# Adding the weighted state of one first-level unit in four by an accumulating DMA from GpSimd

## The reference, cut to what matters

```python
def _ssm(x, xw, dtw, dtb, Al, Dv, g, be):
    ...
    dA = jnp.exp(delta[..., None] * A)
    dBx = delta[..., None] * Bs[:, :, None, :] * xt[..., None]
    def step(h, inp):
        da, dbx, c = inp
        h = h * da + dbx
        return (h, jnp.einsum('bdn,bn->bd', h, c))      # sum over the 16 states n
    ...
    y = ys.transpose(1, 0, 2) + xt * Dv
    return _layernorm(y, g, be)
...
y1 = _ssm(fx1, ...1) + flip(_ssm(flip(fx1), ...2)) + y1_
```

## Time and profile before

| | |
|---|---|
| median of 3 executions | 4336.49 us (4335.89 to 4338.08) |
| profiled execution | 4338.19 us, of which 4336.4 us lie between the first and the last instruction |
| busy share | PE 71%, DVE 82%, ACT 59%, POOL 77% |
| mean granted clock of TensorE | 0.825 |

### The profile page before, as it was taken

One profiled execution on the slowest core, in us unless ns is written; L12 is line 12 of the kernel. 1 busy time (PEld: TensorE's weight loads), 2 busy tenths in 40 slices (PEclk: granted clock), 3 DMA queues, 4 the chain that ended last, 5 costly groups with the idle time before them and its releaser, 6 DMA issues.

```text
span 4336.4 us, 51200 instructions
## 1 busy us (share of the span) xinstructions
PE 3086.1 (71%) x11852; PEld 1449.5 (33%) x11852; DVE 3559.6 (82%) x4199; ACT 2552.1 (59%) x6006; POOL 3338.1 (77%) x1908
## 2 busy tenths in 40 slices
PE   6977767777776778767777876777877777876511
PEld 3433333333332433333333333333333333332200
DVE  2178888888888888888888888888888888898777
ACT  4466665655665665666656666665676566565432
POOL 0069597895969879696896969789596996969798
PEclk8988788888888888887888888888887888888755
DMA  1036354463544446354453534446253454635444
GB/s 40 1 125 206 117 179 147 157 200 108 197 140 157 165 147 204 115 190 146 157 186 125 201 129 167 149 159 209 99 196 131 168 174 137 205 113 182 165 157 174
DMA packets 187260, 663.95 MB, mean 153 GB/s; under 512 B 22736, under 2 KB 24672, under 8 KB 186976
## 3 DMA queue, kind: packets, MB, share of 16 engines
q1 hardware_dynamic: 186976, 661.47, 45.0%
HBM read 639.76 MB, written 21.63 MB: 153 GB/s over the span
## 4 chain that ended last, share of the span: by engine, by line
POOL 28%; issue 23%; DVE 17%; PE 13%; ACT 11%; DMA 6%; DVEq 1%; POOLq 1%; SPq 0%; ACTq 0%
POOL bx L1342 12%; POOL y L1370 7%; DMA bb<-bc_rows 6%; DVE h L581 6%; POOL h L1365 5%; ACT diag L1085 5%; PE pconv L822 4%; DVE slot_c L572 3%; POOL bx L1345 2%; PE pm L848 2%; DVE rs L528 1%; DVE rs L520 1%; ACT slot_b L1200 1%; PE pm L839 1%; POOL delta L1310 1%
## 5 line engine op out<-in xcount | busy, mean ns | idle before, releaser
L822 PE MATMUL pconv<-pad,diag 128*128 128x512 f16 x8064 | 2052.6, 412 | 132.7 <-DVE xn L506 66.9
L1370 POOL TENSOR_TENSOR y<-y,h 128x1024 f32<-128x1024 f32 (+2 forms) x672 | 1335.6, 1987 | 153.9 <-DVE h L581 131.2
L1200 ACT ACTIVATE slot_b<-delta,nega 128x512 f32<-128x512 f32 (+1 forms) x1280 | 804.3, 640 | 1010.6 <-DVE slot_c L572 1009.0
L822 PEld LDWEIGHTS pconv<-pad,diag 128*128 128x128 f16 x8064 | 826.1, 104 | 1328.6 <-issue 423.3
L1342 POOL TENSOR_TENSOR bx<-bb,u 128x1024 f32<-128x1024 f32 x512 | 1219.4, 2382 | 19.9 <-DMA bb<-bc_rows 19.9
L572 DVE TENSOR_TENSOR_SCAN slot_c<-slot_b,bx 128x512 f32<-128x512 f32 (+1 forms) x1024 | 954.2, 956 | 296.1 <-POOL bx L1342 255.4
L581 DVE TENSOR_TENSOR h<-slot_c,cb 128x512 f32<-128x512 f32 x1280 | 860.4, 673 | 36.6 <-POOL y L1370 36.6
L572 DVE TENSOR_TENSOR_SCAN slot_c<-slot_b,slot_c,bx 128x512 f32<-128x512 f32 x512 | 663.7, 1296 | 74.8 <-ACT slot_b L1200 18.7
L1310 POOL TENSOR_TENSOR delta<-delta,rs 128x512 f32<-128x512 f32 (+1 forms) x96 | 111.8, 1164 | 464.6 <-DVE rs L530 464.6
L1365 POOL TENSOR_TENSOR h<-h 128x512 f32<-128x512 f32 (+3 forms) x384 | 361.2, 941 | 98.3 <-DVE h L551 80.7
L1085 ACT ACTIVATE diag<-id,chi 128x128 f16<-128x128 f16 x1344 | 426.6, 386 | 10.7 <-PE pconv L822 10.1
(11 more groups left out here) (168 smaller groups left out, 3555.2 us busy)
## 6 DMA issues: line engine op xcount, KB each, us to landing
bb<-bc_rows SPq DMA_DIRECT2D x592, 512.0 KB, 4.5
cb<-bc_rows SPq DMA_DIRECT2D x592, 512.0 KB, 4.4
xr<-in_x SPq DMA_DIRECT2D x16, 1024.0 KB, 4.9
out<-ob SPq DMA_DIRECT2D x16, 1024.0 KB
bc_rows<-rows SPq DMA_DIRECT2D x64, 64.0 KB, 1.6
w<-in_w SPq DMA_DIRECT2D x2, 256.0 KB
wc<-in_wc SPq DMA_DIRECT2D x2, 256.0 KB
bc_rows<-rows SPq DMA_DIRECT2D x16, 32.0 KB, 1.5
```

Of the source, the lines that this page charges most:

```text
L822: ins = nc.tensor.matmul(bank(pconv, k), w, pad[:, t, part, rows:rows + 16, dx:dx + W], start=first and m == 0, stop=last and m == 2)
L1200: ins = nc.scalar.activation(slot_b[:, o:o + w], delta[:, so + c:so + c + w], ACT.Exp, scale=nega[:, st, n0 + n:n0 + n + 1])
L1370: pool.tensor_tensor(yv, yv, src[:, 0] if len(src.shape) == 3 else src, ALU.add).then_inc(q_y.sem, 1)
```

## The change

In units 6, 10, 14, 18, 22, 26, 30 and 34 (states 1, 5, 9 and 13 of each direction) POOL no longer makes the pass L1370. In its place it issues a DMA from the `h` slot to `ob[:, d, :]`: a plain copy for state 1, an accumulating one (`accum_op=add`) for states 5, 9 and 13. Before it POOL waits for the weighing as before, and for the DMA of four units earlier (for the first of an image: for the store of `ob` of the image before, a wait that DVE's `output` loses). Each of these two waits is carried by an increment of a semaphore of its own. DVE's `weigh` waits for the DMA's arrival where the slot three products back was sent. `norm_centre` of the first level waits for the DMAs too, and subtracts the mean of both sums: a second product, of `ob`, is accumulated onto that of y.

```diff
+def by_dma(q):
+    u, _ = PRODUCTS[q]
+    return UNITS[u][0] == 1 and UNITS[u][3] % 4 == 1
+def added(q):
+    return sum(not by_dma(v) for v in range(q))
+def sent(q):
+    return sum(by_dma(v) for v in range(q))
...
-        q_y = Count("q_y", NP)
+        q_y = Count("q_y", added(NP))
+        q_acc = Count("q_acc", 16 * sent(NP))
...   # DVE, weigh
                 if p == 0 and q >= HR:
-                    dve.wait_ge(q_y.sem, q_y.at(i, q - HR + 1))
+                    if by_dma(q - HR):
+                        dve.wait_ge(q_acc.sem, q_acc.at(i, 16 * sent(q - HR + 1)))
+                    else:
+                        dve.wait_ge(q_y.sem, q_y.at(i, added(q - HR + 1)))
...   # DVE, output
-                if hh == 0:
-                    dve.wait_ge(ob_free.sem, ob_free.at(i + 1, 0))
...   # PE, norm_centre
-                nc.tensor.matmul(o, cen[:, :], src, start=True, stop=True).then_inc(n_yc.sem, 1)
+                    nc.tensor.matmul(o, cen[:, :], src, start=True, stop=True).then_inc(n_yc.sem, 1)
+                    return
+                pe.wait_ge(q_acc.sem, q_acc.at(i, 16 * sent(NORM_NEEDS[k])))
+                nc.tensor.matmul(o, cen[:, :], src, start=True, stop=False)
+                nc.tensor.matmul(o, cen[:, :], ob[:, d, c0:c0 + n], start=False, stop=True).then_inc(n_yc.sem, 1)
...   # POOL, gather
+                if by_dma(q):
+                    pool.wait_ge(q_pr.sem, q_pr.at(i, weighed(q)))
+                    pool.sem_inc(pool_held, 1)
+                    if sent(q) == 0:
+                        pool.wait_ge(ob_free.sem, ob_free.at(i + 1, 0))
+                        pool.sem_inc(pool_held, 1)
+                        pool.dma_start(ob[:, d, :], h[:, q % HR, 0:ln]).then_inc(q_acc.sem, 16)
+                    else:
+                        pool.wait_ge(q_acc.sem, q_acc.at(i, 16 * sent(q)))
+                        pool.sem_inc(pool_held, 1)
+                        if UNITS[k][3] == 1:
+                            pool.dma_start(ob[:, d, :], h[:, q % HR, 0:ln]).then_inc(q_acc.sem, 16)
+                        else:
+                            pool.dma_start(ob[:, d, :], h[:, q % HR, 0:ln], accum_op=ALU.add).then_inc(q_acc.sem, 16)
+                    return
```

More of the change, by code:

```diff
@@ L281, in build @@
         sp_held = sem("sp_held")
+        pool_held = sem("pool_held")
         ch_out = [Count(f"ch_out{n}", 16 * (NCH // 2)) for n in range(2)]
@@ L873, in norm_centre @@
                     pe.wait_ge(n_o.sem, n_o.at(i, STEPS[k]))
-                pe.wait_ge(q_y.sem, q_y.at(i, NORM_NEEDS[k]))
+                pe.wait_ge(q_y.sem, q_y.at(i, added(NORM_NEEDS[k])))
                 o = norm_psum(k)[0][:, 0:cols]
@@ L1368, in gather @@
                 if q:
-                    pool.wait_ge(q_y.sem, q_y.at(i, q))
+                    pool.wait_ge(q_y.sem, q_y.at(i, added(q)))
                 pool.tensor_tensor(yv, yv, src[:, 0] if len(src.shape) == 3 else src, ALU.add).then_inc(q_y.sem, 1)
```

## The result

The changed kernel takes 4381.5 us (median of 4 executions, 4371.96 to 4388.93) against 4336.19 us before (4333.34 to 4338.08): 1.0104 times the time before, 95% interval 1.0083 to 1.0125. It is 45 us slower where 45 us faster was predicted. The profiled execution took 4384.01 us, 4382.2 of it between the first and the last instruction, at a mean granted clock of 0.826 (0.825 before).

The account below looks back on a forecast made before the run. POOL was taken to set the pace from unit 17 to 31, and the chain to norm 4's root in the bridge. 16 images x (2.7 - 5.5) = -45 us gave 4293, 4292 for a median; range 4247 to 4375.

Parts of the forecast that it names:

- What bounds the kernel: Units 17 to 31: POOL sets the pace, busy 63.92 of 64.00 us; in the bridge, DVE waits for norm 4's root.
- The price of a send, c = 1.3 us: On POOL: waiting, two semaphore increments and issuing the DMA cost 1.3 us, the middle between 0.39 and 2.35.
- s: On POOL: time saved per sent gather, 2.3 - 1.3 = 1.0 us.
- rival 1: On POOL: a cheap issue of 0.4 to 0.8 us, saving 1.5 to 1.9 per send; 4247 to 4267 us, chance 0.18.
- Where the saving reaches DVE, 5.5 us per image: 1.0 us each behind gathers 6, 18, 22 and 26, 1.5 behind gather 14, nothing behind 30 and 34.
- the 24 credited to L520: DVE's L520 beside gather 14 falls from 2.19 to 0.68 us, so 1.5 us per image count.
- 3.0 us were credited to gathers 18, 22 and 26: DVE's scans wait behind these gathers, so the saving of 1.0 us counts at each.
- The second sum, 2.7 us per image in the bridge: Bridge, PE ahead of spread 4: direction 1's two products cost 1.8 to 3.6 us, middle 2.7; direction 0's cost nothing.
- The slot of h, "just hidden": From gather 18 to unit 21's first weighing: issue and landing take 7.3 us of the 7.56 available.
- a sign that it is wrong: DVE's weighing waiting for the DMA, a gap of 2 us or more, or no growth of the wait before L625.
- The load of bb, left to the range: POOL's next rows: needed 5.9 us after issue behind a sent gather, median landing 4.5; possible delay left to the range.
- Rival 2: At DVE's weighing: the DMA lands after 8 us, not 6; stalls of 96 us, time 4388 us, chance 0.2.

## Why the prediction was wrong, point by point

1. **What bounds the kernel**: right as far as it went. POOL set the pace, and without sends the relief is worth 87 us.
2. **The price of a send, c = 1.3 us**: too high. The accumulate takes 0.87 us of POOL, the copy 0.60. At gather 18 the next pass begins 0.60 us after the send (time order of POOL above) and takes 0.27 us longer than the one before it. So s is 2.3 - 0.87 = 1.4 rather than 1.0, just under the 1.5 to 1.9 of rival 1. This error alone would have made the kernel faster than forecast, not slower.
3. **Where the saving reaches DVE, 5.5 us per image**: the places early in the image were right, the late ones were eaten. Take the image whose count starts at the norm step of 1541.42 (before: 1526.64). DVE after is ahead of before by 0.5 us ahead of the first send and by 2.2 us at weighing 24, so gather 6 gave 1.7, credited 1.0. L538 behind gather 14 takes 0.68 us at 1664.53 where L520 took 2.19, as predicted; but just ahead of it 1.75 us had been lost where DVE waited for chunk 4 (2.38 us for ACT at 1660.04). That wait comes from PE's clock. PE's products for this chunk, first after and then before:

```profile
1653.61 1.91 PE L882 MATMUL pm<-f,wbc 128*32 128x512 f32 x2 [3.75 <-DVE o L631]
1641.02 1.05 PE L863 MATMUL pm<-f,wbc 128*32 128x512 f32 x2 [1.19 <-DVE o L610]
```

After 3.75 us of idling they run at a granted clock of 0.50, after 1.19 us at 1.00. At this place it is so in 14 of 16 images after and in 2 before, and DVE's wait behind it is 33.7 us in sum instead of 12.6: 21 us that no term of the prediction has, nearly the 24 credited to L520. By weighing 44 the lead is 1.94 us. From there on 3.0 us were credited to gathers 18, 22 and 26; instead DVE lost 3.4 and stood 1.44 behind at the last weighing. The run without sends shows too that the credit was generous: with the whole 2.35 us saved it gave 5.5 us, not the 9 that my way of counting gives.
4. **The second sum, 2.7 us per image in the bridge**: the way was right, the size a little high. Centre 4 to norm 4 grew from 8.56 us to 10.09, the mean over 16 bridges by 1.7 us and that of the whole bridge by 2.0, the wait before the norm step from 57.6 to 84.0 us (101 was written). The run without products puts all four at 48 us against 43, but for direction 0 nothing was counted; 23 of the 57 us by which the span fell without products lie outside the bridge, so a small cost may stand there, and the nearness of the two sums is in part luck.
5. **The slot of h, "just hidden"**: failed. The estimated landing was 6.0 us, the real one 8.4, and the forecast named 7 us as the point from which it decides. The estimate started from the median load of bb, and where few or no loads start in the same moment it holds: 5.3, 5.9 and 5.0 us in three kernels. What it missed is that the end of one bx pass starts both transfers. DVE's wait for the arrival, which the prediction had named as a sign that it is wrong, came to 47.0 us. The price was at most about 38 us by the fourth slot, which holds a part that is not the sends' (above), and 44 by the plain copy, which also saves 0.27 us of POOL in 96 sends.
6. **The load of bb, left to the range**: this is the step that failed most. The prediction had all its numbers: issued at the end of a pass, needed 5.9 us later behind a sent gather, landing 4.5 in the median and 7.2 at most. It asked what added traffic does on average, and not what starts at the same time. The load beside a send took 7.0 us in the median of 104 (6.84 and 7.86 in the lines above), POOL's wait for bb went from 19.9 to 151.2 us, and the third buffer gave back 87 us, against 13 where there were no sends.

So what bounds the kernel, the bridge and L520 stood, and c erred to the safe side; steps 5 and 6 are what turned -45 into +45. Rival 2, the late arrival, came within 7 us of the time (4388, chance 0.2), but by half the mechanism and so in part by luck: it priced the slot, at 96 us where DVE waited 47, and not the load. The range ended at 4375, 6.5 us short, since the load of bb had no price of its own in it.

The rule that stood beside rival 2 (the Trainium skill, Collectives: The Full Stack, section The bandwidth ceiling: in a collective's ring an add in the DMA path reads two sources and so runs at about half a copy's rate) is not borne out in that size by the landings: 8.4 us with the add, 7.0 without it, a fifth more. A landing is not a rate, so the rule itself is not tested by this. Its direction was right, and here the step from 7.0 to 8.4 was enough, because the slot's limit lay between them.

What stays open: how the 87 us of the third buffer divide between its waits (it cut POOL's for bb and DVE's for the slot together) and between fewer common starts and more lead; and how much of the fourth slot's 38 us is the sends'.

## What to carry to other kernels

For each transfer that is added, ask which event starts it and what else that same event starts: here the end of one POOL pass released a load and a send, and they landed after 7.0 and 8.5 us in the median, where a load took 4.5 before. A wait is moved together with all that is queued behind it, so clearing the collision by order cost more than it gave, while a third buffer, which unhooks the load from the pass, gave back 87 us. Work added to a latency path did best in an idle gap next to dense work of its engine: moving two products from the end of the chain into the gap gained 58 us, more than leaving all four out (48).

## What the runs showed of the hardware

- An accumulating DMA of 512 KB costs POOL 0.87 us to issue, a plain one 0.60 us (medians of 96 and 16), well under the 2.35 us pass that it replaced.
- A 512 KB load on SP's queue and a 512 KB send within SBUF, issued within 0.5 us of each other, land after 7.0 and 8.5 us in the median (104 pairs). With the load some 3 us behind the send (the send ahead of the pass) the send lands after 5.9 us, and a load that overlaps it after 4.6.
- The two POOL passes behind an accumulating send lengthen: 2.48 and 2.58 us in the median of 96 in the changed kernel, against 2.36 behind a plain copy (2.63 and 2.62 in the lines of gather 18).
- On PE the same pair of product pieces takes 2.02 us at a granted clock of 0.50 (1794.47, in a stretch that began with 3.41 us of idling) and 1.02 us at 1.00 right behind convolution products (1501.99), the two levels of its clock.
